# The stage between two attentions written out as a pipeline over chunks, with its bf16 splits moved from GpSimd to ScalarE and TensorE

## The reference

```python
x = x + attention0(layernorm(x)); x = x + fp4_ffn(layernorm(...))   # layer 0
# layer 1, attention with convolved keys
kc    = conv1d(xn, Wconv, stride=3)                # 341 rows of a batch
k_tmp = concat([xn[:, :1], kc])                    # 342 keys
q, k, v = xn @ Wq.T, k_tmp @ Wk.T, k_tmp @ Wv.T
p = softmax(q k^T / sqrt(8) + mask); o = p v @ Wo.T + bo
# layer 1, experts
scores = sigmoid(xn @ gate_w + bias); top 2 of 8 experts, gates normalised
```

## Time and profile before

| what | value |
|---|---|
| three runs, us | 1302.80, 1303.87, 1305.22 (median 1303.87) |
| profiled execution, us | 1305.71 |
| its span, us | 1304.0 |
| mean granted TensorE clock, share of 2.4 GHz | 0.926 |
| busy share PE / PEld / DVE / ACT / POOL | 86 / 47 / 75 / 57 / 39 % |
| the stage between the attentions | from 699 to 825.8 us of the span |
| PEclk in slices 22 to 27 of 40 (tenths) | 7 7 6 5 9 9 |

### The profile page before, as it was taken

One profiled execution on the slowest core, in us unless ns is written; L12 is line 12 of the kernel. 1 busy time (PEld: TensorE's weight loads), 2 busy tenths in 40 slices (PEclk: granted clock), 3 DMA queues, 4 the chain that ended last, 5 costly groups with the idle time before them and its releaser, 6 DMA issues. The chain is left out here.

```text
span 1304.0 us, 22545 instructions
## 1 busy us (share of the span) xinstructions
PE 1127.9 (86%) x7455; PEld 619.1 (47%) x7458; DVE 971.5 (75%) x2126; ACT 740.4 (57%) x1143; POOL 509.9 (39%) x778
## 2 busy tenths in 40 slices
PE   4768879999999999999996755799999969999983
PEld 2436653444333434443433433444444438888862
DVE  8979978788888888888842533777777646777788
ACT  3657531666666656665664322166656557777762
POOL 6002220323233323332212526176666661566663
PEclk9889995999999999999987776599999989999997
DMA  4322970013121213120000121012222153678452
GB/s 130 97 79 68 129 85 18 26 38 126 34 75 50 91 35 99 38 94 27 2 2 1 54 76 44 23 48 64 58 64 63 38 178 110 189 235 241 152 130 65
DMA packets 94975, 103.51 MB, mean 79 GB/s; under 512 B 17217, under 2 KB 72838, under 8 KB 94864
## 3 DMA queue, kind: packets, MB, share of 16 engines
q1 hardware_dynamic: 88928, 93.09, 26.4%
q0 software_dynamic: 4992, 8.48, 1.9%
q10 hardware_dynamic: 944, 0.54, 0.2%
HBM read 64.67 MB, written 38.43 MB: 79 GB/s over the span
## 5 line engine op out<-in xcount | busy, mean ns | idle before, releaser
L1112 ACT ACTIVATE a_probs<-a_pst 128x1024 f32<-128x1024 f32 (+4 forms) x544 | 414.4, 813 | 284.5 <-PE a_pst L1060 284.0
L1136 DVE TENSOR_REDUCE a_tops<-a_ps 128x1 f32<-128x512 f32 (+9 forms) x624 | 341.4, 590 | 92.4 <-PE a_ps L1030 84.1
L976 POOL TENSOR_SCALAR_AFFINE_SELECT a_probs<-a_probs 128x256 f32<-128x256 f32 (+3 forms) x384 | 179.8, 480 | 387.3 <-ACT a_probs L1112 382.6
L1030 PE MATMUL a_ps<-kp,qp 96*128 96x512 bf16 (+9 forms) x1280 | 292.8, 307 | 0.8 <-DVE a_tops L1136 0.4
L1060 PE MATMUL a_pst<-qp,kp 99*128 99x512 bf16 (+4 forms) x1088 | 260.7, 332 | 22.6 <-DMA qp<-a_top_rows 18.9
L1079 PE MATMUL a_po<-a_probs,vh 128*32 128x512 f32 (+4 forms) x2176 | 233.1, 501 | 2.0 <-POOL a_probs L976 1.9
L1136 DVE TENSOR_REDUCE a_tops_lead<-a_ps 128x1 f32<-128x512 f32 x256 | 161.8, 683 | 5.7 <-PE a_ps L1030 5.4
L1027 PE MATMUL a_ps<-mask_s,identb 128*128 128x128 bf16 (+8 forms) x624 | 144.3, 234 | 7.0 <-PEq L1220 4.5
L1030 PEld LDWEIGHTS a_ps<-kp,qp 96*128 96x128 bf16 x1280 | 111.9, 101 | 79.1 <-DVE a_tops_lead L1136 15.3
L1060 PEld LDWEIGHTS a_pst<-qp,kp 99*128 99x128 bf16 (+1 forms) x1088 | 92.1, 100 | 120.1 <-ACT a_probs L1112 48.4
L1678 POOL DMA_INDIRECT chosen_rows<-e_slot_y,e_slot_x x92 | 93.4, 1015 | 87.9 <-DVE e_slot_y L1866 60.3
(11 more groups left out here) (269 smaller groups left out, 1715.7 us busy)
## 6 DMA issues: line engine op xcount, KB each, us to landing
e_slot_w<-weight_parts SPq DMA_DIRECT2D x23, 1024.0 KB
weight_parts<-a_cut SPq DMA_DIRECT2D x18, 512.0 KB, 3.1
qp<-q_parts SPq DMA_DIRECT2D x64, 96.0 KB
slot_rows<-empty_row SPq DMA_DIRECT2D x4, 1495.0 KB, 27.3
e_slot_x<-slot_rows SPq DMA_DIRECT2D x23, 260.0 KB, 5.4
a_raw<-in_wraw SPq DMA_DIRECT2D x18, 256.0 KB, 3.7
qp<-q_parts SPq DMA_DIRECT2D x64, 64.0 KB
q_parts<-o SPq DMA_DIRECT2D x24, 128.0 KB
```

The source lines that it names most:

```text
L976: pool.affine_select(out=seen, in_=seen, compare_op=ALU.is_ge, fill=0.0, base=m0, pattern=[[0, 2], [1, mw]], channel_multiplier=-1 if laye ...
L1030: last = pe.matmul(bank[:, i * room:i * room + w], sb["qp"][slot][0:KROWS, j, f["qt"] * P:(f["qt"] + 1) * P], sb["kp"][slot][0:KROWS, j // ...
L1112: act.activation(probs[local % RING][0:st["rows"], 2 * part:2 * part + 2, st["off"]:CHUNK], p_st[part][0:st["rows"], :, st["off"]:CHUNK], ...
L1136: dve.tensor_reduce(out, scores, AX.X, ALU.max).then_inc(s["banks_read"], 1)
```

## The change

`between_layers` is written out: no hardware loop; every engine runs through steps i = -4 to 9, and in step i turns the output of chunk i+4, projects i+3, adds i+2, normalises i+1, turns and queries chunk i, and takes the parts off chunk i-1. The batch that ended with chunk i-1 gets its convolution, keys, values, sigmoid and choice in even steps 2, 4, 6 and 8; the rest of its key split is in the step after. Three SBUF copies go (`stage_o` L1429, `save` L1435, `rows` L1396): the transposes read `o` directly, `xnt` is now `big` itself, and normalising writes into `rows`. The split is done as in the first projection, in two query banks; the logits share the bank of the values. GpSimd keeps the roots alone. SP loads one unit in the stage (after the stores of batch 1), one at the start of the second attention, and two behind the first two `turn_max`.

```diff
 @@ attention, sync
             if layer == 1:
                 store_q1(sp, sb, dram, B - 1, 1)
                 store_k1(sp, sb, dram, B - 1)
-                sp.wait_ge(sb["counts"]["between"]["q_stored"], START + STORES * CHUNKS)
+                load_operands(sp, sb, dram, layer, geo.keys, 0, 1)
+                for par in range(2):
+                    sp.wait_ge(sb["counts"]["between"][f"q_stored{par}"], START + STORES * CHUNKS // 2)
...
+                    if layer == 1 and n + 2 < GROUPS:
+                        load_operands(sp, sb, dram, layer, geo.keys, 0, n + 2)
 @@ between_layers
+        TURN, PROJECT, ADD, NORMALISE = 4, 3, 2, 1
+        steps = range(-TURN, CHUNKS + 2)
+        ended = lambda i: i // 2 - 1 if i >= 2 and i % 2 == 0 else None
+        lagged = lambda i: (i - 1) // 2 - 1 if i >= 3 and i % 2 == 1 else None
 @@ sync
-            store_q1(sp, sb, dram, 0, 0)
-            store_q1(sp, sb, dram, 0, 1)
-            store_k1(sp, sb, dram, 0)
-            sp.wait_ge(s["q_stored"], START + STORES * 2)
-            sp.wait_ge(s["k_stored"], START + STORES)
-            for g in range(GROUPS):
-                load_operands(sp, sb, dram, 1, KEYS1, 0, g)
-            with sp.Fori(1, B - 1) as b:
-                store_q1(sp, sb, dram, b, 0)
-                store_q1(sp, sb, dram, b, 1)
-                store_k1(sp, sb, dram, b)
-            store_q1(sp, sb, dram, B - 1, 0)
+            for b in range(B):
+                for c in range(2):
+                    if 2 * b + c < CHUNKS - 1:
+                        store_q1(sp, sb, dram, b, c)
+                if b < B - 1:
+                    store_k1(sp, sb, dram, b)
+                if b == 1:
+                    for par in range(2):
+                        sp.wait_ge(s[f"q_stored{par}"], START + STORES)
+                    sp.wait_ge(s["k_stored"], START + STORES)
+                    load_operands(sp, sb, dram, 1, KEYS1, 0, 0)
 @@ tensor
+            def take_off_q(n, part, copied):
+                pe.wait_ge(s[copied], START + n + 1)
+                pe.matmul(p_q[n % 2][:, :], sb["minus_identb"][:, :], q_parts[n % 2][:, part, :], start=False, stop=True,
+                          skip_group_check=True).then_inc(s["rests_done"], 1)
...
+            for i in steps:
+                if is_chunk(i):
+                    turn_xn(i)
+                if is_chunk(i - 1):
+                    take_off_q(i - 1, 0, "heads_done")
+                if ended(i) is not None:
+                    convolve(ended(i))
+                if lagged(i) is not None:
+                    take_off_k(lagged(i), 0, "k_heads_done")
+                if is_chunk(i + PROJECT):
+                    project(i + PROJECT)
+                if is_chunk(i):
+                    query(i)
+                    route(i)
+                if is_chunk(i - 1):
+                    take_off_q(i - 1, 1, "middles_done")
+                if ended(i) is not None:
+                    keys_values(ended(i))
+                if lagged(i) is not None:
+                    take_off_k(lagged(i), 1, "k_middles_done")
+                if is_chunk(i + TURN):
+                    turn_o(i + TURN)
             rank()
 @@ scalar
+            def head_q(n):
+                act.wait_ge(s["q_projected"], START + n + 1)
+                if n >= 2:
+                    act.wait_ge(s[f"q_stored{n % 2}"], START + STORES * (n // 2))
+                act.activation(q_parts[n % 2][:, 0, :], p_q[n % 2][:, :], ACT.Copy).then_inc(s["heads_done"], 1)
+
+            def rest_q(n, part, copied):
+                act.wait_ge(s["rests_done"], START + 2 * n + part)
+                act.activation(q_parts[n % 2][:, part, :], p_q[n % 2][:, :], ACT.Copy).then_inc(s[copied], 1)
...
+            for i in steps:
+                if is_chunk(i):
+                    copy_xn(i)
+                if ended(i) is not None:
+                    sigmoid(ended(i))
+                if is_chunk(i - 1):
+                    rest_q(i - 1, 1, "middles_done")
+                if ended(i) is not None:
+                    copy_convolved(ended(i))
+                if lagged(i) is not None:
+                    rest_k(lagged(i), 1, "k_middles_done")
+                if is_chunk(i):
+                    head_q(i)
+                if is_chunk(i - 1):
+                    rest_q(i - 1, 2, "tails_done")
+                if ended(i) is not None:
+                    head_k_copy_v(ended(i))
+                if lagged(i) is not None:
+                    rest_k(lagged(i), 2, "k_tails_done")
+                if is_chunk(i + TURN):
+                    copy_o(i + TURN)
 @@ vector
+            for i in steps:
+                if ended(i) is not None:
+                    logits(ended(i))
+                if is_chunk(i + NORMALISE):
+                    normalise(i + NORMALISE)
+                if is_chunk(i + ADD):
+                    add(i + ADD)
+                if ended(i) is not None:
+                    choose(ended(i))
             place_tokens()
```

More of the change, by code:

```diff
@@ L1245, in between_layers @@
         RS = 1 + 2 * BT + 8
-        X = sb["x"]
-        block = ctx.enter_context(nc.Block())
[L1249 to L1259, removed]
+        X, xnt = sb["x"], sb["big"]
@@ L1266, in root @@
                 pool.wait_ge(s["root_steps"], START + 2 * n + 1)
-                pool.tensor_tensor(rstd[:, :], var[:, :], sb["minus_half"][:, 0:CT], ALU.pow)\
+                pool.tensor_tensor(rstd[:, tiles(n)], var[:, tiles(n)], sb["minus_half"][:, 0:CT], ALU.pow)\
                     .then_inc(s["root_steps"], 1)
[L1270 to L1288, removed]
         @block.sync
         def _(sp):
-            store_q1(sp, sb, dram, 0, 0)
@@ L1321, in project, with turn_xn @@
                 last.then_inc(s["projected"], 1)
-            def chunk(following, n, b, c, more=False):
-                if following is not None:
-                    turn_o(following)
+            def turn_xn(n):
                 pe.wait_ge(s["xn_ready"], START + CT * (n + 1))
+                if n:
+                    pe.wait_ge(s["xnt_copied"], START + n)
                 for t in range(CT):
-                    last = pe.transpose(p_xn[:, t * P:(t + 1) * P], xn[:, t * P:(t + 1) * P], sb["ident"][:, :])
+                    last = pe.transpose(p_xn[:, t * P:(t + 1) * P], sb["rows"][:, n * CT + t, 0:E], sb["ident"][:, :])
@@ L1353, in batch @@
                     .then_inc(s["k_projected"], 1)
-                pe.wait_ge(s["v_copied"], START + 2 * b)
                 for t in range(KT):
@@ L1415, in batch, with rest_k @@
                 rows = KEYS1 - full * P
-                act.activation(sb["v1"][0:rows, bass.ds(b * KT + full, 1), :],
-                               p_v[0:rows, full * P:(full + 1) * P].rearrange("p (t f) -> p t f", f=P), ACT.Copy)\
+                act.activation(sb["v1"][0:rows, b * KT + full, :], p_v[0:rows, full * P:(full + 1) * P], ACT.Copy)\
                     .then_inc(s["v_copied"], 1)
+            def rest_k(b, part, copied):
+                act.wait_ge(s["k_rests_done"], START + 2 * b + part)
+                act.activation(k_parts[:, part, :], p_k[:, 0:KEYS1], ACT.Copy).then_inc(s[copied], 1)
@@ L1471, in batch, with logits @@
-            def batch(b):
-                step, base = s["router_steps"], RS * b
+                for t in range(n * CT, (n + 1) * CT):
+                    dve.tensor_scalar(sb["rows"][:, t, 0:E], X[:, t, :], mean[:, t:t + 1], rstd[:, t:t + 1],
+                                      ALU.subtract, ALU.mult).then_inc(s["xn_ready"], 1)
+            def logits(b):
                 dve.wait_ge(s["logits_done"], START + 2 * b + 2)
-                dve.tensor_tensor(logit[:, :, :], p_r[:, 0:BT * EXPERTS].rearrange("p (t e) -> p t e", e=EXPERTS),
+                dve.tensor_tensor(logit[:, :, :], routed.rearrange("p (t e) -> p t e", e=EXPERTS),
@@ L1538, in _ @@
             dve.memset(sb["hot_sum"][:, TILES:TILES + 1, :], 0.0)
-            stage_o(0)
-            normalise(0, lambda: stage_o(1))
-            run(dve, chunk, batch)
+            for i in steps:
[7 more added lines that the diff above has]
+                    choose(ended(i))
             place_tokens()
```

196 lines of the change are left out of this document (91 added, 105 removed).

## The result

The changed kernel takes 1269.61 us (median of 4 runs, 1267.14 to 1271.34), the kernel before, run beside it on the same chip, 1304.55: a ratio of 0.973, 95% interval 0.9705 to 0.9756. That is 34.9 us less, where 27.5 were forecast.

The account below looks back on a forecast made before the run. The stage between the attentions was taken as bound by latency, engines waiting for each other. Stage -35.9, second attention's start +7.7 and +0.7 sum to -27.5 us: from a median of 1303.87 to about 1276.5 us, range 1264 to 1293.

Parts of the forecast that it names:

- the likeliest case: The forecast itself: whole kernel at about 1276.5 us, 27.5 us less; chance 0.63, own range 1270 to 1285.
- Part 1: Start of the stage between the attentions: dropping the staging copy of `o` gains 0.5 us, bounds 0 and 1.
- Part 2: Pipeline steps: 0 and 1 set by stores, 11.8 us; 2 to 5 by TensorE, 15.1 us per two, 30.2 together.
- Part 3: Stage's stall: SP's 12 operand loads delay ScalarE's head of chunk 6; some 10 of the old hole's 16 us return.
- Part 4: Stage's end after chunk 7's head: 9.2 us, ranking and slots 8.1, hand-overs 1.3; second attention starts 35.9 us earlier.
- Part 5: Second attention's start: unit 1's first fill waits 7.7 us for SP's loads; 0.7 us more for later units.
- Rival (a): Stage: more is won, without the 10 us stall or with TensorE at full clock to the end; 1266.5 us; chance 0.17.
- Rival (b): Steps 2 to 5: TensorE at the half clock, 21 us more; 1295.5 us; chance 0.13.
- Rival (c): Second attention's start: three late groups of loads each delay a unit; slower, about 1308.5 us; chance 0.04.
- (d): Stage: no overlap, 24 us a batch as before, only the hole shrinks, 16 to 10; about 1302 us; chance 0.03.

Follow-up runs that it names:

- e1: The changed kernel with unit 0's 12 operand loads issued behind chunk 6's stores instead of behind the keys of batch 1; 1257.18 us, ratio 0.9638.
- e3: The changed kernel with all 48 operand loads put back behind batch 0's stores, as in the kernel before; 1289.24 us, ratio 0.9877.
- e5: The changed kernel with unit 0's loads in fours behind chunks 3 to 5's stores, unit 1's halved between chunk 6's stores and the attention's start; 1252.90 us.
- e7: e5 with the split put back on GpSimd; 1255.05 us, ratio 0.9626.
- e10: e8 with the keys split by GpSimd and the queries still by ScalarE and TensorE; 1247.76 us, ratio 0.9552.
- e8: e5 with three query part buffers instead of two; 1250.51 us, ratio 0.9581.
- e6: The changed kernel with the split put back on GpSimd, pipeline and SP's order kept; 1268.00 us, ratio 0.9722.
- e2: The changed kernel with the loads of units 0 and 1 behind chunk 6's stores and none at the second attention's start; 1259.38 us, ratio 0.9661.
- e9: The kernel before with the hardware loops of all engines written out and nothing else changed; 1301.66 us, ratio 0.997.

## Why the prediction was right

The forecast of 1276.5 us missed by 6.9, in the likeliest case and on its mechanisms: the hole at chunk 6 for the 12 loads, then the late fill of unit 1. The profiled executions missed by more, 1278.2 against 1267.91: the one before lay above its median and the one after below it. By its steps:

- **Part 1, the head.** First normalised chunk ready 9.14 us after the last `o` against 10.17: 1.0 us, where I took 0.5. Missed: chunk 0's turn starts only at 710.20, 3.4 us after that. Chunk 2's projection stands ahead of it in TensorE's queue and waits 1.25 us for VectorE's add, and behind that the turn of chunk 3's output; both run at the half clock (0.50 from 697 to 710.2 us), 2.04 us for a projection that takes 1.06 at the full one.
- **Part 2, the steps.** This is the term that was mis-sized. Two steps took 12.1 us (turn of chunk 2 at 720.48, of chunk 4 at 732.59) and 11.7, not 15.1. I added durations; but matmuls of neighbouring groups overlap, and what counts is the time from start to start: 0.44 for a turn of 0.60, 0.22 for a subtraction of 0.38, 0.86 for a query of 1.02. Over steps 2 to 5 that is 30.2 - 23.8 = 6.4 us, the largest single error. Steps 0 and 1 took 10.3 us (710.20 to 720.48), not 11.8, which made up for half of the late start. In steps 2 to 5 the full clock came as forecast (1.00), and so did the normalising: 1.11 or 1.12 us in every chunk.
- **Part 3, the stall.** From the last key tail to chunk 6's head 761.31 - 746.46 = 14.9 us, forecast 15.5; wait 11.96, forecast some 10; head of chunk 7 another 5.47, forecast 5.8. Right, and e1 shows that the loads' place is its cause. Counted from the last `o` it began 2.8 us earlier than forecast (48.8 against 51.7) and not 6.4: 1.4 us were lost by the start of step 2, and the keys' last copy comes 2.2 us after chunk 6's turn (744.24), where I had put the two at one time.
- **Part 4, the end.** Head of chunk 7 to the ranking 8.8 us, forecast 9.2. From there to the slots 6.3, forecast 8.1: I had taken the old end over unchanged, but its 32 matmuls ran at the lower clock then (3.75 us) and at the full one now (2.05). From the slots to the first fill it was 0.3 us, where I took 1.3 for hand-overs and barrier.
- **Part 5, the attention's start.** Unit 1's fill came 13.7 us after the start, forecast 15.45: the last load landed 1.4 us after its issue ended, not 2.7, which was the landing of stores. Unit 0's maxima were sent 798.32 - 782.19 = 16.1 us after the start against 10.8 before, so 5.3 us later, forecast 7.7. The fills of units 2 and 3 waited for no load.

The stage was forecast at 91.6 us (790.0 - 698.43) and took 84.6. Of the 7.0 us, steps 2 to 5 gave 6.4, the stall and what follows it 1.4, the ranking and slots 1.8, the hand-overs 1.0; the start of step 2 (1.4) and the keys' last copy (2.2) took back 3.6. The attention's start gave another 3.1 (8.4 forecast, 5.3 measured).

The stage and its start together: 84.6 + 5.3 against 127.4, 37.5 us less, and the spans of the two profiled executions differ by 37.8. The medians differ by 34.9, because the profiled execution before lay 1.2 us above the median beside it and the one after 1.7 below.

Rival (a), 1266.5, was nearer in its number (3.1 off against 6.9) but wrong in its reason: the stall that it left out was there, 11.96 us. The forecast's own number is partly luck: errors of opposite sign met in it (3.6 us taken back, above). Rival (b) asked for the half clock in steps 2 to 5, where 1.00 was granted. The clock was low at two other places: 0.50 from 697 to 710.2 us, behind an attention that ended at 1.00 and gaps of 0.94 and 0.69 us, and 0.50 from 761.9 to 768.2, behind the 9.64 us of idleness. The Trainium skill's rule on waits for DMAs between matmuls (TensorE: Matmul & The Clock Gate, HAM oscillation) agrees with the second place; at the first TensorE waited for no DMA. Rival (c) asked for late units 2 and 3, which did not come. (d) fell with the first two steps.

The Trainium skill's rule that I set against Part 5, to issue a DMA early and wait on it late (DMA: Bandwidth & Descriptors, Rules for kernel authors), was tried whole in e3: no fill waits, and the kernel is 19.6 us slower than the changed one, so here the measurement decides against it. The place between the two, e5, is 16.7 us faster. SP's rows show why: twelve issues take 8.7 us of the queue that the stores need too.

What isn't settled: whether the new split is worth anything by itself (e5 against e7, 2.2 us, intervals overlap); whether e10 gains on e8 at all, and if so how much by the clock and how much by the order (both changed at once); and what the three SBUF copies that went were worth. No run puts them back. They were busy 3.4, 3.4 and 5.0 us in the stage before (L1429, L1435, L1396), 11.8 in all on VectorE and ScalarE; how much of it lay on the path is not shown, so "the pipeline" above takes them in.

## What to carry to other kernels

A queue that only issues DMAs is an engine with a length: here 0.72 us for each load, and here its order decided more than which engine does the arithmetic (moving the loads on SP gave another 16.7 us on top of the change, changing the engines of the split some 2 or less). Put transfers that are needed later in small groups between those that someone waits for now, put no long run of them ahead of a store whose buffer is wanted back, and none that is still being issued when a barrier is due. When a pipelined engine's steps are summed, take start-to-start times from a stretch in which it does not idle.

## What the runs showed of the hardware that was not expected

- The same ranking matmuls took 2.05 us in the changed kernel and 3.63 in e8, with a granted clock of 1.00 against 0.57 on average; an end after a stretch of waits should be priced at both levels.
- At the stage's head the granted clock fell from 1.00 (690 to 697 us) to 0.51 (697 to 703) without a long wait, in the changed kernel; before, it was 0.50 there too (699 to 712).
- VectorE's normalising took 1.11 us alone and 1.85 to 2.35 beside GpSimd's split (e6).
- Loads from DRAM landed 1.4 us after their issue ended, stores about 2.4 us after (an estimate: 761.31 - 757.10, less 1.8 for the issue of chunk 4's three parts, whose row is merged with chunk 5's).
- The barrier at a block's end waits for every engine and for SP's queue. TensorE stood there 4.5 us with only VectorE's slots left to do, 13.9 and 15.4 where SP (e2) or GpSimd (e6) was behind. From VectorE's last instruction to the first fill it was 0.3 us (781.87 to 782.19).
- Written out (e9), the stage needs one table load of 1.28 us where the hardware loop held two in each of three iterations.
